# Reordered waits inside the head pairs, a spread of the side work, and identity products on TensorE in its idle stretches

## The chip, the cores and the metric

One core of a Trainium2 chip. The metric is the device time of the kernel in microseconds (us), the median of its runs. TensorE is the matmul engine (PE in the profile, PEld its weight loads), DVE is VectorE, ACT is ScalarE, POOL is GpSimd, SP is SyncE, which here only issues transfers.

## The reference

`x` is [4, 1024, 128] in float32. The block computes `x = x + attn(layernorm(x))`, where attn itself adds its input, and then `x = x + ffn(layernorm(x))`:

- attention: 16 heads of 64, `softmax(q k^T / 8) v` over 1024 keys for each batch and head, then the output projection, added to the normed input
- feed-forward: a mixture of 8 experts. `probs = softmax(x Wr)`, each of the 4096 tokens goes to its best expert, at most 512 tokens an expert in order of token number, `y = relu(xe W1) W2` times the token's probability (of the tokens of the second layernorm, which the branch adds to its result). Tokens beyond the 512 keep zero

```python
q = einsum('bsd,hdk->bhsk', x, w_q)      # k, v likewise
weights = softmax(einsum('bhqk,bhmk->bhqm', q, k) * scale, axis=-1)
z = einsum('bhqm,bhmk->bhqk', weights, v)
x = x + einsum('bse,ed->bsd', z, w_o)
rank = cumsum(onehot(argmax(probs))) ...  ; keep = rank < cap
```

## The kernel before, in words

**Tiling.** Two heads make a pair: 4 batches x 8 pairs = 32 pairs (`PAIRS`), walked in order by every engine (`in_order`, L243). A pair has 4 octets (`oct`); an octet is 8 tiles of scores (k = 0 to 7), each 128 keys x 512 queries of one head. Octets 0 and 1 are the first 512 queries (h = 0), octets 2 and 3 the second 512. For each tile TensorE makes the scores in one of three banks ps_s (`scores`, L1004 and L1005: two products, high and low parts), ScalarE writes the exponential into `ring` (`unit`, L583), GpSimd adds the tiles up over keys into `acc` (`add_up`, L444, one add of 128x1024 for two tiles), and TensorE multiplies the ring by V into ps_z (`values`, L1018) and later sums `acc` over partitions (`softmax_sums`, L1028).

**The maximum.** Before a pair's scores are used, the maximum over keys must be known: TensorE makes a cheap copy of the scores (`max_scores`, L970, called a visit, two per octet, numbered v) into the four banks of ps_m, DVE reduces them (`reduce_max`, L783), TensorE turns the maxima (`turn_max`, L989), ScalarE copies them to mxt (L563) and SP places them as a row of queriesB (`place_max`, L315). A visit uses all of ps_m, so everything else that needs PSUM borrows a part of ps_m between two visits and must be read out before the next: lent_qk (projections of q and k for the next pairs), lent_turn, lent_out (V's projection and the output projection), lent_max. In the code of TensorE the waits of those readers stand together in front of the visit (L1116 to L1138).

**The side work of an octet**, all inside the same order: `project_qk` (L949 to L951), `cast_qk` (ACT, L542), `low_qk` (DVE, L778), `place` (SP, L302 to L309), `project_v` and `copy_v` (L958, ACT L558) in octets 0 and 2, `project_out` (L1036) and `add_out` (DVE, L805) in octets 1 and 3, `recip` (DVE, L792, four quarters), `scale_z` (DVE, zT, L800). `split_high_weights` (ACT, L546) stands once in each pair, behind octet 0.

**Rarer work.** The tokens of a batch are split into a high and a low part (`split_high_tokens` on ACT L553, `split_low_tokens` on POOL L432) two pairs before the batch starts, in pairs 6, 14 and 22. `clear_slots` (ACT's queue, L529) fills the table of slots in HBM, in pair 1. The routing of batches 0 to 2 is spread over the pairs from 23 on by `routed(j, role)`, for batch b in pairs 23+2b (a: moments), 24+2b (b: second norm), 25+2b (c: turn, logits, choose, count_ranks, find_slots), 26+2b (d) and 27+2b (e: scatter of the rows, POOL L420, an indirect DMA for each 128 tokens). Batch 3 is routed behind the last pair. Then the experts follow (L1196 to L1234).

**Where the order comes from.** Everything is written out by hand: each engine's list of instructions in `pair(j, par, b)`, with semaphores that count.

```python
                    unit(j, oct, 3)
                    if oct in (0, 2) and not last:
                        copy_v(j + 1, nxt, oct // 2, lent_out)
                    unit(j, oct, 4)
```

Before the pairs, DVE finds the moments of batches 0 and 1, norms batch 0, sets constants and norms batch 1 (L713 to L722); the moments of batches 2 and 3 come right in front of the pairs (L873).

Of the kernel before, what the change touches and what calls it, by code (L numbers as in the profile page):

```python
# [28 lines left out]
def block_kernel(nc, x_in, w_q, w_k, w_v, w_o, w_r, w_1, w_2, out):  # L29
# [30 lines left out]
    with ExitStack() as ctx:  # L60
# [167 lines left out]
        def qk_bank(j, use):  # L228
            if isinstance(j, int) and j == 0:
                return ps_m[1 - use // 2][:, (use % 2) * HALF:(use % 2 + 1) * HALF]  # L230
            if isinstance(j, int) and j == 1 and use < 2:
                return ps_s[use][:, :]
            return lent_qk
# [3 lines left out]
        LAST_BY_PE = 2  # L237
        LAST = PAIRS - 1


        LOOPED = []

        def in_order(engine, pair):  # L243
            j = 0
            while j < PAIRS:
                looped = dict(LOOPED).get(j)
                if looped:
                    with engine.Fori(0, looped) as i:
                        for par in range(2):
                            pair(2 * i + j + par, par, j // HP)  # L250
                    j += 2 * looped
                else:
                    pair(j, j % 2, j // HP)
                    j += 1
# [6 lines left out]
        def routed(j, role):  # L261
            if not isinstance(j, int):
                return None
# [3 lines left out]
        def known(j, *which):  # L267
            return isinstance(j, int) and j in which

        @block.sync  # L270
        def _(sp):
# [5 lines left out]
            def load_weights(j, par):  # L277
                hp = j % HP
                view = wst[par][:, 0:4 * DK].rearrange("p (h t k) -> p h t k", h=2, t=2)
                sp.dma_start(view[:, :, 0, :], wq_d[:, bass.ds(2 * hp, 2), :]).then_inc(w_loaded[par], 16)  # L280
                sp.dma_start(view[:, :, 1, :], wk_d[:, bass.ds(2 * hp, 2), :]).then_inc(w_loaded[par], 16)
                sp.dma_start(wst[par][:, 4 * DK:6 * DK].rearrange("p (h k) -> p h k", h=2),
                             wv_d[:, bass.ds(2 * hp, 2), :]).then_inc(w_loaded[par], 16)
            def load_wo(j, par):
                sp.dma_start(wo[par][:, :].rearrange("p (o d) -> p o d", o=1),
                             wo_d[:, bass.ds(j % HP, 1), :]).then_inc(wo_loaded[par], 16)
# [78 lines left out]
        def _(pool):  # L365
# [64 lines left out]
            def split_low_tokens(b):  # L430
                pool.wait_ge(high_split, 2 * b + 2)
                pool.tensor_tensor(h_low[:, :], hT[:, b * S:(b + 1) * S], h_high[:, :].bitcast(F32),  # L432
                                   ALU.subtract).then_inc(low_split, 1)

            def add_up(j, h, kt):
                pool.wait_ge(exp_done, 2 * UNITS * j + UNITS * h + 2 * kt + 2)
                if kt == 1:
                    if not (isinstance(j, int) and j == 0):
# [818 lines left out]
```

## Time and profile before

| | |
|---|---|
| median of 3 runs | 1662.51 us (1659.98 to 1663.33) |
| the profiled execution, its own time | 1658.69 us |
| its span | 1656.9 us |
| TensorE busy (PE) | 1524.6 us, 92% |
| weight loads (PEld) | 870.7 us, 53% |
| VectorE, ScalarE, GpSimd busy | 1072.0 (65%), 811.3 (49%), 1189.6 us (72%) |
| the chain that ended last | PE 85%, DVE 4%, POOL 3% |
| mean granted clock of TensorE | 0.963 of full speed |

A page of the profile gives one execution: busy times, the costliest groups of instructions, and for each the idle time of its engine in front of them. The trace behind it can be asked for single instructions in order of time, for waits summed by pairs of lines, and for busy times in chosen stretches.

### The profile page before, as it was taken

The page shows a single profiled execution, that of the slowest core. Times are in us where ns is not written, and L with a number is a line of the kernel's source. Part 1 is how long each engine was busy: PE and PEld are TensorE (multiplying, and loading weights), DVE is VectorE, ACT ScalarE, POOL GpSimd, SP SyncE. Part 2 cuts the span into 40 slices and gives each one's busy share as a digit, 9 for nine tenths or more (in the row PEclk, how much of TensorE's full clock was granted, in tenths as well). Part 3 has the DMA queues.
Part 4 walks back from the last instruction along what each step waited for, and adds up shares of the span by engine and source line. Part 5 has one row for each costly group of instructions (what it writes and reads, how often), then busy time and mean ns, then how long its engine had stood idle before and what let it go on. Part 6 is the DMA issues. An engine that isn't in the chain of part 4 may idle for free.

```text
span 1656.9 us, 21749 instructions
## 1 busy us (share of the span) xinstructions
PE 1524.6 (92%) x7396; PEld 870.7 (53%) x7396; DVE 1072.0 (65%) x1316; ACT 811.3 (49%) x1586; POOL 1189.6 (72%) x687
## 2 busy tenths in 40 slices
PE   3798999999999999999999999999998989999376
PEld 1354555555555555555555555555564555554266
DVE  4665676666766666756677666667677767766332
ACT  1464555545455455455555555454554645545221
POOL 2586677777777777777777777777877868879225
PEclk8799999999999999999999999999999989999588
DMA  5345222333333332223333332322233322220531
GB/s 136 78 117 128 56 66 64 73 79 80 80 81 70 74 79 68 63 50 78 80 80 81 80 78 67 80 60 65 63 70 90 96 64 70 71 70 25 155 126 37
DMA packets 115342, 129.56 MB, mean 78 GB/s; under 512 B 40490, under 2 KB 65583, under 8 KB 115232
## 3 DMA queue, kind: packets, MB, share of 16 engines
q1 hardware_dynamic: 108512, 117.80, 30.3%
q0 software_dynamic: 2560, 6.14, 1.1%
q10 hardware_dynamic: 4160, 4.23, 1.1%
q8 instruction: 60, 0.98, 0.3%
q14 instruction: 50, 0.41, 0.1%
HBM read 18.91 MB, written 12.65 MB: 19 GB/s over the span
## 4 chain that ended last, share of the span: by engine, by line
PE 85%; DVE 4%; POOL 3%; ACT 2%; issue 2%; DMA 2%; SPq 1%; POOLq 0%; DVEq 0%; ACTq 0%
PE ps_z L1018 26%; PE ps_s L1004 15%; PE ps_s L1005 13%; PE ps_m L970 10%; PE ps_m L958 3%; PE ps_s L1028 3%; PE ps_m L1036 3%; ACT ring L583 2%; PE ps_m L949 2%; PE ps_m L950 2%; PE ps_m L951 2%; DVE mxw L783 1%; POOL acc L444 1%; PE ps_m L1211 1%; PE ps_z L1211 1%
## 5 line engine op out<-in xcount | busy, mean ns | idle before, releaser
L444 POOL TENSOR_TENSOR acc<-acc,ring 128x1024 f32<-128x1024 f32 x382 | 907.0, 2374 | 189.1 <-ACT ring L583 148.7
L783 DVE TENSOR_REDUCE mxw<-ps_m 128x1 f32<-128x1024 f32 x512 | 602.7, 1219 | 425.7 <-PE ps_m L970 424.0
L583 ACT ACTIVATE ring<-ps_s 128x512 f32<-128x512 f32 x1024 | 544.9, 600 | 122.5 <-PE ps_s L1005 120.7
L1018 PE MATMUL ps_z<-ring,V 128*64 128x512 f32 x2048 | 471.2, 602 | 0.0
L1004 PE MATMUL ps_s<-queriesA,keysA 128*128 128x512 f32 x1024 | 441.5, 431 | 16.7 <-ACT ring L583 13.8
L1005 PE MATMUL ps_s<-queriesB,keysB 65*128 65x512 f32 x1024 | 409.8, 400 | 0.0
L1018 PEld LDWEIGHTS ps_z<-ring,V 128*64 128x64 f32 x2048 | 136.6, 137 | 268.8 <-issue 240.4
L1004 PEld LDWEIGHTS ps_s<-queriesA,keysA 128*128 128x128 f32 x1024 | 196.3, 192 | 126.6 <-issue 48.0
L444 POOL TENSOR_TENSOR acc<-ring 128x1024 f32<-128x1024 f32 x64 | 152.8, 2388 | 145.0 <-ACT ring L583 145.0
L792 DVE RECIPROCAL sums<-sums 128x128 f32<-128x128 f32 x252 | 228.9, 930 | 8.7 <-ACT sums L574 8.7
L970 PE MATMUL ps_m<-keysA,queriesA 64*128 64x512 f32 x1024 | 190.9, 450 | 26.9 <-DVE mxw L783 9.8
L1005 PEld LDWEIGHTS ps_s<-queriesB,keysB 65*128 65x128 f32 x1024 | 197.0, 192 | 32.2 <-issue 0.8
L970 PEld LDWEIGHTS ps_m<-keysA,queriesA 64*128 64x128 f32 x1024 | 78.5, 188 | 179.3 <-issue 153.6
L574 ACT ACTIVATE sums<-ps_s 128x512 f32<-128x512 f32 x63 | 37.7, 598 | 266.2 <-PE ps_s L1028 266.2
L569 ACT ACTIVATE zr<-ps_z 128x512 f32<-128x512 f32 x64 | 38.3, 598 | 223.2 <-PE ps_z L1018 223.2
L778 DVE TENSOR_TENSOR qk_rest<-ps_m,qk_high 128x512 fp32r<-128x512 f32 x126 | 85.8, 682 | 46.8 <-ACT qk_high L542 29.8
L542 ACT ACTIVATE qk_high<-ps_m 128x512 fp32r<-128x512 f32 x126 | 75.4, 599 | 43.0 <-PE ps_m L951 23.0
L1036 PEld LDWEIGHTS ps_m<-wo,zT 128*128 128x128 f32 x512 | 67.8, 194 | 11.8 <-issue 6.0
L1036 PE MATMUL ps_m<-wo,zT 128*128 128x128 f32 x512 | 68.7, 277 | 4.3 <-DVE zT L800 4.3
L958 PEld LDWEIGHTS ps_m<-wst,hT 128*128 128x128 f32 x496 | 69.1, 202 | 6.2 <-DVE mxw L783 0.2
L958 PE MATMUL ps_m<-wst,hT 128*128 128x128 f32 x496 | 69.1, 285 | 0.0
L1028 PE MATMUL ps_s<-acc,ones 128*64 128x512 f32 x256 | 66.7, 593 | 0.0
(126 smaller groups left out, 916.6 us busy)
## 6 DMA issues: line engine op xcount, KB each, us to landing
queriesA<-qk_high SPq DMA_DIRECT2D x256, 128.0 KB, 2.3
keysB<-qk_high SPq DMA_DIRECT2D x128, 128.0 KB, 2.3
keysA<-qk_rest SPq DMA_DIRECT2D x128, 128.0 KB, 2.4
queriesB<-qk_rest SPq DMA_DIRECT2D x128, 128.0 KB, 2.4
keysA<-qk_high SPq DMA_DIRECT2D x96, 128.0 KB, 2.3
tokens_by_slot<-blank ACTq DMA_DIRECT2D x4, 1032.0 KB, 7.5
ring<-tokens_by_slot SPq DMA_DIRECT2D x8, 516.0 KB, 6.2
x<-in_L_attn_x SPq DMA_DIRECT2D x4, 512.0 KB, 6.4
```

The costliest lines, as they stand in the source:

```text
L444: pool.tensor_tensor(acc[h][:, :], before, P_both(kt), ALU.add).then_inc(summed, 1)
L583: act.activation(P_tile(kt, p), ps_s[k % 3][:, :], ACT.Exp, scale=SCALE).then_inc(exp_done, 1)
L778: dve.tensor_tensor(qk_rest[s][:, :], qk_bank(j, use), qk_high[s][:, :].bitcast(F32), ALU.subtract).then_inc(qk_low, 1)
L783: dve.tensor_reduce(mxw[h][:, p * HT + qt:p * HT + qt + 1], ps_m[p][:, :], AX_X, ALU.max).then_inc(maxed, 1)
L792: dve.reciprocal(sums[:, c], sums[:, c]).then_inc(recip_done, 1)
L958: mm = pe.matmul(bank[:, i * P:(i + 1) * P], hT[:, t:t + P], wst[par][:, 4 * DK:6 * DK], start=True, stop=True)
L970: mm = pe.matmul(ps_m[p][:, kh * HALF:(kh + 1) * HALF], queriesA[par][p][r, at:at + P], keysA[par][p][r, kh * HALF:(kh + 1) * HALF], start ...
L1004: pe.matmul(ps_s[k % 3][:, :], keysA[par][p][:, t], queriesA[par][p][:, c], start=True, stop=False)
L1005: pe.matmul(ps_s[k % 3][:, :], keysB[par][p][:, t], queriesB[par][p][:, c], start=False, stop=True).then_inc(scores_ready, 1)
L1018: mm = pe.matmul(ps_z[p * DK:(p + 1) * DK, :], V[par][:, kt * P + p * DK:kt * P + (p + 1) * DK], P_tile(kt, p), start=(kt == 0), stop=(kt ...
L1028: mm = pe.matmul(ps_s[2][p * DK:(p + 1) * DK, :], ones[:, :], part, start=(i == 0), stop=(i == len(parts) - 1))
L1036: mm = pe.matmul(bank[:, i * P:(i + 1) * P], zT[h][:, i * P:(i + 1) * P], wo[par][:, :], start=True, stop=True)
```

## The change

On TensorE: `spin(times)` multiplies the identity by itself into ps_s[1], 20 times before the first turn, 18 times behind the last sums, 38 times in front of the wait for the last output projection's add, 70 times behind the last batch's ranks. In the pairs:

- ACT: unit 4 comes before copy_v
- DVE: add_out comes before the second quarter of recip; `find_slots` (and TensorE's `count_ranks`) go from octet 3 of the pair with role c to octet 0 of the pair with role d, their second part behind that octet's reductions
- the tokens of a batch are split in two halves: behind octets 0 and 2 on ACT, in front of the add of kt = 5 of either half on POOL
- `clear_slots`: 16 stores of 256 rows in pairs 3 to 6 in place of 4 of 1024 rows in pair 1
- POOL: the 8 scatters of a batch stand 4 in the second half of role d and 4 in the first half of role e; before, 6 in d and 2 in e
- DVE: the moments of batch 2 come before the norm of batch 0, those of batch 3 behind it

A form with loops that was not in use is taken out. The diff, cut:

```diff
         LAST_BY_PE = 2
+        CLEAR_FROM, CLEARED = 3, 2 * P
...
+        SPLIT_IN = {0: 0}
+        SPLIT_IN.update((HP * b - 2, b) for b in range(1, B))
...
-                    pool.wait_ge(slots_cleared, 16 * (E * CAP // S))
+                    pool.wait_ge(slots_cleared, 16 * (E * CAP // CLEARED))
...
-            def split_low_tokens(b):
-                pool.wait_ge(high_split, 2 * b + 2)
-                pool.tensor_tensor(h_low[:, :], hT[:, b * S:(b + 1) * S], h_high[:, :].bitcast(F32),
+            def split_low_tokens(b, g):
+                pool.wait_ge(high_split, 2 * b + g + 1)
+                c, at = slice(g * HALF, (g + 1) * HALF), b * S + g * HALF
+                pool.tensor_tensor(h_low[:, c], hT[:, at:at + HALF], h_high[:, c].bitcast(F32),
                                    ALU.subtract).then_inc(low_split, 1)
...
-                        if known(j, 0) and (h, kt) == (0, 6):
-                            split_low_tokens(0)
-                        if known(j, *range(HP - 2, PAIRS - HP, HP)) and (h, kt) == (1, 1):
-                            split_low_tokens(b + 1)
+                        if j in SPLIT_IN and kt == 5:
+                            split_low_tokens(SPLIT_IN[j], h)
...
-                        if routed(j, "d") is not None and kt in (3, 5, 7):
-                            scatter(routed(j, "d"), [3 * h + kt // 2 - 1])
-                        if routed(j, "e") is not None and h == 0 and kt in (3, 5):
-                            scatter(routed(j, "e"), [6 + kt // 2 - 1])
+                        if routed(j, "d") is not None and h == 1 and kt % 2 == 1:
+                            scatter(routed(j, "d"), [kt // 2])
+                        if routed(j, "e") is not None and h == 0 and kt % 2 == 1:
+                            scatter(routed(j, "e"), [4 + kt // 2])
...
-            def split_high_tokens(b, last_use):
-                act.wait_ge(hT_ready, 2 * b + 2)
-                act.wait_ge(qk_done, last_use)
-                for g in range(2):
+            def split_high_tokens(b, g):
+                act.wait_ge(hT_ready, 2 * b + g + 1)
+                if b > 0:
+                    act.wait_ge(qk_done, 4 * HP * b - 2 + 2 * g)
...
                     unit(j, oct, 3)
+                    unit(j, oct, 4)
                     if oct in (0, 2) and not last:
                         copy_v(j + 1, nxt, oct // 2, lent_out)
-                    unit(j, oct, 4)
...
-                    if known(j, 0) and oct == 0:
-                        split_high_tokens(0, 0)
-                    if oct == 1 and known(j, *range(HP - 2, PAIRS - HP, HP)):
-                        split_high_tokens(b + 1, 4 * (j + 1) + 4)
+                    if j in SPLIT_IN and oct in (0, 2):
+                        split_high_tokens(SPLIT_IN[j], oct // 2)
...
-                    if known(j, 1):
-                        clear_slots(oct)
+                    if CLEAR_FROM <= j < CLEAR_FROM + E * CAP // CLEARED // OCTS:
+                        clear_slots(OCTS * (j - CLEAR_FROM) + oct)
...
-            for b in range(2):
+            for b in range(3):
                 for g in range(2):
                     first_moments(b, g)
             for g in range(2):
                 first_norm(0, g)
+            for g in range(2):
+                first_moments(3, g)
...
+                    if oct in (1, 3) and not first:
+                        add_out(j - 1, oct // 2, before, lent_out)
                     if oct == 1 and not first:
                         recip(j - 1, 1, 1)
-                        add_out(j - 1, 0, before, lent_out)
                     if oct == 3:
                         recip(j, 0, 1)
-                        if not first:
-                            add_out(j - 1, 1, before, lent_out)
...
-                    if routed(j, "c") is not None and oct == 3:
-                        find_slots(routed(j, "c"), 0)
+                    if routed(j, "d") is not None and oct == 0:
+                        find_slots(routed(j, "d"), 0)
...
-                    if routed(j, "c") is not None and oct == 3:
-                        find_slots(routed(j, "c"), 1)
+                    if routed(j, "d") is not None and oct == 0:
+                        find_slots(routed(j, "d"), 1)
...
-            for b in (2, 3):
-                for g in range(2):
-                    first_moments(b, g)
...
+            def spin(times):
+                for _ in range(times):
+                    pe.matmul(ps_s[1][:, 0:P], ident[:, :], ident[:, :], start=True, stop=True)
...
-                    pe.wait_ge(low_split, b + 1)
+                    pe.wait_ge(low_split, 2 * b + half + 1)
...
-                    if c is not None and oct == 3:
-                        count_ranks(c)
+                    if routed(j, "d") is not None and oct == 0:
+                        count_ranks(routed(j, "d"))
...
+            spin(20)
             for g in range(2):
                 turn_h(0, g)
...
             softmax_sums(LAST, 1, LAST_BY_PE)
+            pe.wait_ge(exp_done, UNITS * HALVES)
+            spin(18)
             project_out(LAST, 1, 1, lent_qk)
 
+            spin(38)
             pe.wait_ge(wo_added, 2 * PAIRS)
...
             count_ranks(B - 1)
+            spin(70)
```

## Rows read from the trace of the kernel before

**Rows 1.** List of waits: who waited for whom, us in total, times, longest.
```profile
PE ps_s L1004 <- ACT ring L583: 13.8, 51, 1.8
...
PE ps_m L970 <- issue: 7.7, 26, 0.3
```

**Rows 2.** Timeline, pair 4, octet 0: start us, us, engine, line, out<-in [idle before].
```profile
250.58 0.60 ACT L558 ACTIVATE V<-ps_m 128x512 f32<-128x512 f32 x1 [0.66 <-PE ps_m L958]
...
251.10 0.39 PE L1005 MATMUL ps_s<-queriesB,keysB 65*128 65x512 f32 x1
...
251.72 0.50 PE L1004 MATMUL ps_s<-queriesA,keysA 128*128 128x512 f32 x1 [0.23 <-ACT ring L583]
```

**Rows 3.** Timeline, pair 4, octet 1.
```profile
262.58 0.94 DVE L792 RECIPROCAL sums<-sums 128x128 f32<-128x128 f32 x1
...
263.44 0.63 DVE L805 TENSOR_TENSOR x<-ps_m,x 128x512 f32<-128x512 f32 x1
...
264.17 0.73 PE L970 MATMUL ps_m<-keysA,queriesA 64*128 64x512 f32 x4 [0.30 <-issue]
```

**Rows 4.** Timeline of ScalarE, the one L546 in pairs 1, 3, 6 and 7.
```profile
109.57 0.44 ACT L546 ACTIVATE w_high<-wst 128x256 fp32r<-128x256 f32 x1
...
207.90 0.45 ACT L546 ACTIVATE w_high<-wst 128x256 fp32r<-128x256 f32 x1
...
343.16 0.45 ACT L546 ACTIVATE w_high<-wst 128x256 fp32r<-128x256 f32 x1
...
391.87 0.45 ACT L546 ACTIVATE w_high<-wst 128x256 fp32r<-128x256 f32 x1
```

**Rows 5.** Timeline of TensorE: the matmuls behind its long pauses in pairs 1, 6, 26 and 30.
```profile
128.71 0.50 PE L1004 MATMUL ps_s<-queriesA,keysA 128*128 128x512 f32 x1 [2.92 <-DMA queriesB<-mxt]
...
362.74 0.58 PE L949 MATMUL ps_m<-h_high,w_low 128*128 128x512 f32 x1 [1.82 <-POOL h_low L432]
...
1256.02 0.79 PE L949 MATMUL ps_m<-h_high,w_low 128*128 128x512 f32 x1 [5.36 <-DVE mxw L783]
...
1453.55 0.50 PE L949 MATMUL ps_m<-h_high,w_low 128*128 128x512 f32 x1 [2.02 <-DVE mxw L783]
```

**Rows 6.** Stretches: us, busy us (count) of each engine, PEclk, DMA share, GB/s.
```profile
1253.80:1260.70 6.90, 4.68 (x16) 4.01 (x16) 4.55 (x7) 1.20 (x2) 2.15 (x2) 0.51 0.29 65
...
1540.60:1588.30 47.70, 13.39 (x56) 10.82 (x57) 13.97 (x47) 10.91 (x23) 12.37 (x25) 0.50 0.47 143
```

**Rows 7.** Timeline, GpSimd's adds and DVE's step beside them, pairs 25 and 30.
```profile
1247.10 7.38 POOL L444 TENSOR_TENSOR acc<-acc,ring 128x1024 f32<-128x1024 f32 x3
...
1252.31 2.19 DVE L768 TENSOR_TENSOR scatter_at<-routing_columns 128x8 int32<-128x8 f32 x1
...
1499.61 4.51 DVE L800 TENSOR_TENSOR zT<-sums,zr 128x512 f32<-128x512 f32 x1
```

**Rows 8.** Timeline, the end of the start.
```profile
52.52 0.88 DVE L694 BATCH_NORM_STATS2 moment_parts<-x 128x6 f32<-128x128 f32 x4
...
57.90 2.32 DVE L783 TENSOR_REDUCE mxw<-ps_m 128x1 f32<-128x1024 f32 x2
...
59.15 2.08 PE L945 MATMUL ps_m<-hT,wst 128*128 128x512 f32 x2 [3.06 <-DVE mxw L783]
```

**Rows 9.** Timeline, the last pair and what follows it.
```profile
1506.49 1.00 POOL L420 DMA_INDIRECT tokens_by_slot<-rows,scatter_at  x1 [0.15 <-POOL acc L444]
...
1523.77 10.18 POOL L444 TENSOR_TENSOR acc<-acc,ring 128x1024 f32<-128x1024 f32 x4
...
1542.08 2.04 PE L1036 MATMUL ps_m<-wo,zT 128*128 128x128 f32 x8 [4.31 <-DVE zT L800]
...
1557.46 3.56 PE L1050 MATMUL ps_m<-wr,hT 128*128 128x8 f32 x16 [0.84 <-ACT hT L496]
...
1582.91 1.09 PE L1201 MATMUL ps_m<-ident,ring 128*128 128x128 f32 x4 [19.42 <-DMA ring<-tokens_by_slot]
...
1593.73 3.73 PE L1211 MATMUL ps_z<-w,rT 128*128 128x128 f32 x32
```

More of the change, by code:

```diff
@@ L228, in qk_bank @@
         def qk_bank(j, use):
-            if isinstance(j, int) and j == 0:
+            if j == 0:
                 return ps_m[1 - use // 2][:, (use % 2) * HALF:(use % 2 + 1) * HALF]
-            if isinstance(j, int) and j == 1 and use < 2:
+            if j == 1 and use < 2:
                 return ps_s[use][:, :]
@@ L237, in block_kernel @@
         LAST_BY_PE = 2
+        CLEAR_FROM, CLEARED = 3, 2 * P
         LAST = PAIRS - 1
-        LOOPED = []
         def in_order(engine, pair):
[L244 to L254, printed above, removed]
+            for j in range(PAIRS):
+                pair(j, j % 2, j // HP)
+        SPLIT_IN = {0: 0}
+        SPLIT_IN.update((HP * b - 2, b) for b in range(1, B))
         ROUTE_FROM = PAIRS - 9
@@ L261, in routed @@
         def routed(j, role):
-            if not isinstance(j, int):
-                return None
             b, odd = divmod(j - ROUTE_FROM - "abcde".index(role), 2)
@@ L267, in known @@
         def known(j, *which):
-            return isinstance(j, int) and j in which
+            return j in which
         @block.sync
@@ L437, in add_up @@
                 if kt == 1:
-                    if not (isinstance(j, int) and j == 0):
+                    if not (j == 0):
                         pool.wait_ge(sums_done, 2 * j + h - 1)
@@ L528, in clear_slots @@
                 act.wait_ge(blank_ready, 2)
[L529 to L530 removed]
+                act.dma_start(slots_d[n * CLEARED:(n + 1) * CLEARED, :].rearrange("(p n) w -> p n w", p=P),
+                              blank[:, :].rearrange("p (o w) -> p o w", o=1).to_broadcast([P, CLEARED // P, W])
                               ).then_inc(slots_cleared, 16)
@@ L774, in low_qk @@
                 s = use % 2
-                if not (isinstance(j, int) and j == 0 and use < 2):
+                if not (j == 0 and use < 2):
                     dve.wait_ge(low_placed[s], 32 * (2 * j + use // 2))
@@ L809, in pair @@
                 first, last = known(j, 0), known(j, LAST)
-                before = (j - 1) // HP if isinstance(j, int) else b
+                before = (j - 1) // HP
                 for oct in range(OCTS):
@@ L964, in max_scores @@
                 at = h * HALF + qt * P
-                if not (isinstance(v, int) and v == 0):
+                if not (v == 0):
                     pe.wait_ge(maxed, 2 * v)
@@ L1067, in pair @@
                 first, last = known(j, 0), known(j, LAST)
-                next_b = (j + 1) // HP if isinstance(j, int) else b
-                second_b = (j + 2) // HP if isinstance(j, int) else b
+                next_b, second_b = (j + 1) // HP, (j + 2) // HP
                 for oct in range(OCTS):
@@ L1130, in pair @@
                             pe.wait_ge(logits_copied, c + 1)
-                        if c is not None and oct == 3:
-                            pe.wait_ge(ranks_read, c + 1)
+                        if routed(j, "d") is not None and oct == 0:
+                            pe.wait_ge(ranks_read, routed(j, "d") + 1)
                         if oct in (1, 3):
```

15 lines of the change are left out of this document (6 added, 9 removed).

## The prediction, made before the changed kernel ran

> **What bounds the kernel now.** I read the page first (its numbers are in the table above): TensorE is busy for 92% of the span and carries 85% of the chain that ended last, so only what lets TensorE start earlier, or run at its higher clock, counts. Then I asked how regular it is. One ScalarE instruction (L546) runs once per pair, at a fixed place; [rows 4] give its starts in pairs 1, 3, 6 and 7. Pairs 3 to 6 follow each other at (343.16 - 207.90) / 3 = 45.09 us. That is the undisturbed pair. Anything above it is a one-off stall, anything inside it is paid some 30 times. So the sum has two kinds of terms: small waits in every pair, and stalls in the few pairs that carry extra work.
>
> **Waits in every pair.** In an octet of 8 score tiles the last one starts 251.72 - 251.10 = 0.62 us after the instruction in front of it, where 0.23 is the step of a 512-column matmul [rows 2]: 0.39 lost. It needs a bank of ps_s whose exponential (unit 4) comes behind copy_v on ScalarE, and ScalarE stood idle 0.66 us in front of copy_v for TensorE's project_v. The list of waits counts 51 such waits [rows 1], one of them (the 1.8) another story, so 50. The change puts unit 4 in front of copy_v. Its scores are ready by then, it fits into the idle 0.66, and copy_v starts when it did. The end of copy_v (251.18) is then the next to be late, but TensorE asks for V only at its visit, 0.8 us later. Unit 5, behind copy_v, keeps its time. Gain 50 x 0.39 = 19.5; nothing at the other end, if something else holds that tile.
>
> In the second octet TensorE waits 0.30 us in front of its visit [rows 3], 26 times in the list [rows 1]. The 263.44 add (add_out) is what it needs, because lent_out is in a bank that the visit overwrites, and a reciprocal of 0.94 stands in front of that add. The change swaps them. The add can then start at 262.6, when the projection has just left TensorE, and ends before TensorE arrives; the reciprocal runs beside the visit (0.73 us and more). With the step lost at its start I count 0.36: 26 x 0.36 = 9.3. In the fourth octet the same swap finds no wait to remove: nothing. The new wait is for wo_done at the head of DVE's queue, with a reciprocal and a reduction behind it; the reduction has to wait for the visit anyway.
>
> **Stalls that go.** (a) clear_slots. Pair 1 issues four stores of 1032 KB from ScalarE's queue; the small move of the maxima into queriesB is then late and TensorE waits 2.92 us [rows 5]. From pair 1 to pair 3 the pitch is 98.33 [rows 4], 8.15 over two undisturbed pairs, the rest being a late placement in pair 2 and the slow clock behind it. The change makes 16 stores of a quarter of the size in pairs 3 to 6. A quarter of 2.92 is 0.7 in four pairs, but in part there is room: I take -8.1 and +1, between +0 and +4. The Trainium skill (Trainium Kernel Development and Optimization, Key Constraints) says that DMAs from several queues interleave on the same engines. By that alone the small move would not have been held up; the 2.92 says that it was.
>
> (b) The token split for the next batch. In pair 6 TensorE stands 1.82 us for h_low [rows 5], which GpSimd makes in one piece right before it is wanted. The pitch to pair 7 is 48.71 [rows 4], 3.62 too long: 1.82 waiting and 1.8 at a granted clock that fell during the pause. The pattern stands three times (pairs 6, 14, 22); once the clock holds. The change makes the first half a whole octet earlier and the second half in time for the next pair: 3 x 1.82 + 2 x 1.8 = 9.1 gone. It costs two more issues on ScalarE and GpSimd, both with room.
>
> (c) Routing of batches 0 to 2. The stall of 5.36 us at 1256.02 [rows 5] comes from DVE: find_slots stands in front of the reduction that TensorE waits for. Its tiny instructions took up to 2.19 us, and this one ended just as the third add of GpSimd's 7.38 us did [rows 7]. During the stall the clock fell: 4.68 us of matmuls at half clock [rows 6], so 2.3 more. This stands in pairs 26 and 28 (7.7 each); in pair 30 it is 2.02 and about 1.7 of clock. Sum 19. The change moves the step behind the visit of the next pair's first octet, where DVE has about 2.8 us until its next reduction while find_slots takes 1.5 us beside an idle GpSimd (in the tail) and 6 beside its adds. Next late is that reduction. Between no stall and 3 us each I take 1.1 each, because GpSimd has a pause of 2 us in that octet, and 1 us for the four scatters per half: -15.7 + 1 = -14.7. Four scatters in a half (before three and two) are otherwise covered by GpSimd's pauses in these pairs. The rule of the skill (SBUF — State Buffer, Who interferes with whom) is that DVE with two SBUF inputs and a GpSimd instruction that reads SBUF exclude each other for a whole instruction. The 2.19 agrees; zT's 4.51 [rows 7], longer than any one add, does not. By the rule three blocks of at most one add each could follow in the new place too, and the saving would be nearer 10.
>
> **Start.** DVE's moments for batches 2 and 3 leave the place before the pairs, where TensorE idles 3.06 us for the reduction at 57.90 [rows 8]. With the clock that fell there I count 3.06 + 1.7 = 4.8. They go in front of the norms of batches 0 and 1. Four halves took 57.90 - 52.52 = 5.38, or 1.35 each; the first two partly fall into DVE's wait for the roots, the others delay the first low_qk. Cost 1.6 us (between 0 and 5). The 20 identity products run in the wait for the first turn. If they keep the clock up, that is lost again in DVE's order: nothing. Sum -3.2.
>
> **Tail.** One product is 2 instructions. At high clock 3.73 / 32 = 0.117, at low clock 3.56 / 16 = 0.22 [rows 9], so 0.23 or 0.44 us a product. 18 of them are 4.2, behind the last sums, where TensorE idles 4.31; 38 are 8.9 in an idle of some 10; 70 are 16.4 (30.8 at low clock) in an idle of 19.42 [rows 9]. Now the clock is low from 1540.6 to 1588.3, with 13.39 us of matmuls [rows 6], of which some 8 lie on the path; half of that could be won. I take 3, between 0 and 4. Against it: GpSimd's adds are unbroken to the end, 1523.77 + 10.18 = 1533.95 [rows 9], when TensorE is ready for the last sums. Two more scatters of 1.0 stand in that row of adds now: +1.9. Net -1.1, between -4 and +10 (70 products at low clock would outlast their wait by about 10).
>
> **Sum.** -19.5 - 9.3 - 7.1 - 9.1 - 14.7 - 3.2 - 1.1 = -64. The profiled execution took 1658.7, so 1594.7; the median of the runs is 3.8 above that execution, so 1598.
>
> **Rivals.**
> - *The waits in every pair only move* (0.17). Another wait stands just behind: the tile's bank comes free and V, the add or a placement holds TensorE instead. For: several semaphores meet at the visit. Against: each is met 0.7 us or more earlier. The 29 us stay: 1627.
> - *Routing still stalls* (0.13). In the new octet find_slots meets GpSimd's adds and delays the reduction by 3 us or more, with the clock falling again. Then 12 of 15.7 stay: 1610.
> - *It does not do what it says* (0.03): the products fail to raise the clock and outlast their waits at 0.44 each; 70 are 11 us over, the other two about 10. With the 3 not won: 1622.
> - *Slower* (0.03). zT is in front of low_qk on DVE, and V's visit waits for low_qk. Once zT took 4.51 us [rows 7] because it met unbroken adds. Bare it is 0.7, so 3.8 late, less 1.5 of room: 2.3 us, twice a pair. If shorter octets bring zT into GpSimd's adds in all pairs, it is +140 and the time is about 1735. It decides when zT starts before GpSimd's last add of the half ends; now a pause of about 1 us lies between.
>
> **How the numbers follow.** Forecast 0.64, at 1598. A change of under 0.2% (3.3 us) can't be told from none. The range runs from the best ends (clears 1, routing 3, start 1.6, tail 3, and 4 for the median) to just short of the first rival: 1586 to 1624. Every case but the last ends faster by more than 3.3 us; for small misses together I leave 0.02 on no change. Faster 0.95, same 0.02, slower 0.03.
>
> **What would show it.** L546 at a pitch of 44.0 in quiet pairs; the L1004 and L970 waits of [rows 1] gone; a step of 0.23 at the last tile; no wait for mxt in pair 1 and none for h_low in 6, 14, 22; the stall in pairs 26 and 28 about 1 us; the last add on GpSimd 2 us later than TensorE; high clock in the tail's routing. I am wrong if the pitch stays near 45, or if TensorE's idle in pairs 24 to 31 is as large as now.

## The result and the profile after

The changed kernel took 1603.09 us (median of 4 runs, 1600.34 to 1604.84) against 1661.24 for the kernel before beside it: a ratio of 0.9648, 95% interval 0.9629 to 0.9666. In a later trial it was 0.9641 (0.9624 to 0.9658). The forecast was 1598.0, range 1586 to 1624. The time lies inside, but one large term of the sum failed, and another, which I had put too small, covered about half of it: the hit is in part luck.

| | before | after |
|---|---|---|
| the profiled execution, own time | 1658.69 us | 1604.84 us |
| span | 1656.9 us | 1602.8 us |
| TensorE busy | 1524.6 us, 92% | 1536.1 us, 96% |
| mean granted clock | 0.963 | 0.975 |

TensorE is busier although it does the same useful work: the identity products count as busy. So the share says little here, and I read waits and single instructions.

From the list of waits of the changed kernel (us in total, times, longest), and from the page the group of the scores' first matmuls, with the idle time in front of them at the end:

```profile
PE ps_m L961 <- DVE mxw L773: 9.8, 4, 2.4
PE ps_m L940 <- DVE mxw L773: 9.5, 3, 4.6
```

```profile
L995 PE MATMUL ps_s<-queriesA,keysA 128*128 128x512 f32 x1024 | 433.3, 423 | 0.4
```

L995 stood 13.8 us for its exponential in [rows 1] (L1004 there); now its whole idle is 0.4. The 26 waits of L970 are gone too. The 9.8 belongs to the start. The 9.5 is the stall of pairs 26, 28 and 30, which was to go.

Timeline, pair 4, octet 0, then octet 1:

```profile
236.51 0.60 ACT L548 ACTIVATE V<-ps_m 128x512 f32<-128x512 f32 x1
...
237.01 0.40 PE L996 MATMUL ps_s<-queriesB,keysB 65*128 65x512 f32 x1
237.24 0.40 PE L995 MATMUL ps_s<-queriesA,keysA 128*128 128x512 f32 x1
237.48 0.40 PE L996 MATMUL ps_s<-queriesB,keysB 65*128 65x512 f32 x1
...
248.00 0.68 DVE L795 TENSOR_TENSOR x<-ps_m,x 128x512 f32<-128x512 f32 x1
248.60 0.94 DVE L782 RECIPROCAL sums<-sums 128x128 f32<-128x128 f32 x1
...
249.24 0.73 PE L961 MATMUL ps_m<-keysA,queriesA 64*128 64x512 f32 x4
```

Beside [rows 2]: the step to the last tile is 0.23 (before 0.62), with 0.24 behind it. Beside [rows 3]: the add comes first and ends 0.56 before the visit, which waits for nothing.

ScalarE's one L536 (L546 before) in pairs 1, 3, 6 and 7:

```profile
106.42 0.42 ACT L536 ACTIVATE w_high<-wst 128x256 fp32r<-128x256 f32 x1
...
194.74 0.42 ACT L536 ACTIVATE w_high<-wst 128x256 fp32r<-128x256 f32 x1
...
326.11 0.42 ACT L536 ACTIVATE w_high<-wst 128x256 fp32r<-128x256 f32 x1
...
369.81 0.42 ACT L536 ACTIVATE w_high<-wst 128x256 fp32r<-128x256 f32 x1
```

Pair 7 follows pair 6 at 43.70 now, where [rows 4] had 48.71: the split of the tokens costs nothing. From pair 1 to pair 3 it is 88.32 (98.33 before). Pairs 3 to 6 stand (326.11 - 194.74) / 3 = 43.79 apart; of the 0.27 us above three times 43.70, 0.2 is in pair 4 alone. Most quiet pairs have 43.70, against the 45.09 of before.

Now the part that failed. Timeline of pair 26, octets 0 and 1: GpSimd, DVE, TensorE; and the stretch behind the pause (us, busy us and count of PE, PEld, DVE, ACT, POOL, then PEclk, DMA share, GB/s):

```profile
1205.68 2.36 POOL L436 TENSOR_TENSOR acc<-acc,ring 128x1024 f32<-128x1024 f32 x1
...
1208.19 2.39 POOL L436 TENSOR_TENSOR acc<-acc,ring 128x1024 f32<-128x1024 f32 x1
...
1211.23 2.33 POOL L436 TENSOR_TENSOR acc<-acc,ring 128x1024 f32<-128x1024 f32 x1
```

```profile
1206.05 2.07 DVE L752 TENSOR_TENSOR logits<-one_hot,logits 128x64 f32<-128x64 f32 x1
1208.15 0.22 DVE L753 TENSOR_REDUCE routing_columns<-logits 128x8 f32<-128x64 f32 x1
1208.41 2.19 DVE L755 TENSOR_SCALAR routing_columns<-routing_columns 128x8 f32<-128x8 f32 x1
...
1210.71 0.57 DVE L757 TENSOR_TENSOR routing_columns<-routing_columns 128x8 f32<-128x8 f32 x1
1211.32 2.26 DVE L758 TENSOR_TENSOR scatter_at<-routing_columns 128x8 int32<-128x8 f32 x1
...
1213.86 2.30 DVE L773 TENSOR_REDUCE mxw<-ps_m 128x1 f32<-128x1024 f32 x2
```

```profile
1215.09 0.79 PE L940 MATMUL ps_m<-h_high,w_low 128*128 128x512 f32 x1 [4.63 <-DVE mxw L773]
```

```profile
1211.00:1221.00 10.00, 5.91 (x18) 4.98 (x19) 7.46 (x10) 2.74 (x6) 4.92 (x3) 0.66 0.16 37
```

Three tiny instructions of find_slots take 2.07, 2.19 and 2.26 us, and each ends within 0.1 us of an add of GpSimd (1208.04, 1210.58, 1213.56). A fourth takes 0.57 and ends as GpSimd's short step for w_low does (1211.26). This part of find_slots lasts 7.9 us, the reduction behind it starts 5 us after its visit has ended, TensorE waits 4.63 us, and its clock is at half from 1214.2 to 1221.0. It is the picture of before [rows 5, 7], one octet later. An octet here is the time from its first exponential to the next octet's first:

| | before | after |
|---|---|---|
| pair 26, octets 0 and 1 | 19.56, 10.91 | 11.62, 18.18 |
| pair 28, octets 0 and 1 | 19.74, 10.92 | 11.63, 17.88 |
| pair 30, octets 0 and 1 | 15.16, 10.92 | 11.65, 11.07 |

The tail, from the last pair to the first tokens:

```profile
1466.57 10.15 POOL L436 TENSOR_TENSOR acc<-acc,ring 128x1024 f32<-128x1024 f32 x4
...
1476.78 1.78 PE L1019 MATMUL ps_s<-acc,ones 128*64 128x512 f32 x2 [0.99 <-POOL acc L436]
...
1482.09 4.29 PE L922 MATMUL ps_s<-ident 128*128 128x128 f32 x36
...
1500.44 3.14 PE L1041 MATMUL ps_m<-wr,hT 128*128 128x8 f32 x16 [0.84 <-ACT hT L486]
...
1525.43 0.63 PE L1196 MATMUL ps_m<-ident,ring 128*128 128x128 f32 x4 [1.16 <-DMA ring<-tokens_by_slot]
```

The unbroken adds end 1.9 us later behind the last exponential than in [rows 9], and TensorE stands 0.99 us for them and 0.80 for zT before. Its clock is low from 1477.0 to 1480.4. From the last exponential to the first tokens it is 54.4 us, 52.7 before. From there to the end it is 77.4 against 74.0, which the experiments settle below.

### The profile page after: what moved, and what is told of

Read it like the earlier page. It is cut to its first block, busy times and chain, and to the rows that moved or that the text cites. A ratio compares the mean times of both kernels' runs of the same rounds, so it can differ in the third digit from the quotient of the medians.

```text
span 1602.8 us, 22351 instructions
## 1 busy us (share of the span) xinstructions
PE 1536.1 (96%) x7688; PEld 904.4 (56%) x7688; DVE 1079.0 (67%) x1316; ACT 811.6 (51%) x1586; POOL 1189.5 (74%) x691
## 4 chain that ended last, share of the span: by engine, by line
PE 86%; DVE 5%; POOL 4%; issue 1%; SPq 1%; DMA 1%; ACT 1%; another core or an unknown queue 0%; POOLq 0%; DVEq 0%; ACTq 0%
PE ps_z L1009 26%; PE ps_s L995 15%; PE ps_s L996 14%; PE ps_m L961 10%; PE ps_m L949 3%; PE ps_s L1019 3%; PE ps_m L1027 3%; POOL acc L436 3%; PE ps_m L940 2%; PE ps_m L941 2%; PE ps_m L942 2%; DVE mxw L773 1%; PE ps_z L1206 1%; POOL tokens_by_slot L411 1%; PE ps_m L1206 1%
## 5 line engine op out<-in xcount | busy, mean ns | idle before, releaser
L995 PE MATMUL ps_s<-queriesA,keysA 128*128 128x512 f32 x1024 | 433.3, 423 | 0.4
L995 PEld LDWEIGHTS ps_s<-queriesA,keysA 128*128 128x128 f32 x1024 | 195.7, 191 | 88.6 <-issue 45.4
L961 PEld LDWEIGHTS ps_m<-keysA,queriesA 64*128 64x128 f32 x1024 | 77.5, 187 | 170.1 <-issue 145.8
L949 PEld LDWEIGHTS ps_m<-wst,hT 128*128 128x128 f32 x496 | 65.5, 192 | 5.9 <-DVE mxw L773 0.2
L949 PE MATMUL ps_m<-wst,hT 128*128 128x128 f32 x496 | 65.8, 275 | 0.0
```

What stands on the lines that cost most here:

```text
L949: mm = pe.matmul(bank[:, i * P:(i + 1) * P], hT[:, t:t + P], wst[par][:, 4 * DK:6 * DK], start=True, stop=True)
L961: mm = pe.matmul(ps_m[p][:, kh * HALF:(kh + 1) * HALF], queriesA[par][p][r, at:at + P], keysA[par][p][r, kh * HALF:(kh + 1) * HALF], start ...
L995: pe.matmul(ps_s[k % 3][:, :], keysA[par][p][:, t], queriesA[par][p][:, c], start=True, stop=False)
```

## The experiments

Twelve kernels ran, 1 to 4 on one chip, 5 to 8 on a second and 9 to 12 on a third. Each is compared with the kernel before on its own chip.

**1. find_slots back at its old place.**

```diff
-                    if routed(j, "d") is not None and oct == 0:
-                        find_slots(routed(j, "d"), 0)
+                    if routed(j, "c") is not None and oct == 3:
+                        find_slots(routed(j, "c"), 0)
```

(and so its second part and count_ranks)

> The changed kernel, but find_slots and count_ranks stand in octet 3 of pair c again, as before the change. The stall did not go with the move: pairs 26 and 28 lost 7.8 and 7.9 us in octet 0 before, and 7.6 and 7.3 in octet 1 after; only pair 30 fell from 3.7 to 0.5. Theory A (the place changes nothing while GpSimd's adds lag there): about 1606 us, that is 3 to 4 slower than the changed kernel, with octet 0 of pairs 26 and 28 at 18.5 to 19.5 and octet 1 at 10.55 again. Rival B (the new place is worse than the old one once the pairs are shorter): 1598 or less. Rival C (the old place is much worse): over 1610.

Measured: 1599.66 us, ratio 0.9639 (0.9623 to 0.9655), that of the changed kernel. Octet 0 of pairs 26 and 28 is 18.98 and 19.28, octet 1 is 10.55 again; pair 30's octet 0 is 13.16. The stall is there at either place: theory A. Over pairs 25 to 30 the octets are 2.9 us longer at the old place (without a dip of the clock in pair 27), which the ratios can't separate from nothing; the median is low because the experts' stretch is 3.4 us shorter on this chip (runs 9 to 11).

**2. No identity products.** The four calls of spin are left out.

> The changed kernel without any identity product (the 20, 18, 38 and 70 are left out, the orders stay). Theory A (the products in the tail are worth their clock): low clock from the last sums to the experts' first tokens, 3 us or more lost in the tail, the start the same within 0.5 us: 1606 to 1608. Rival B (they are worth nothing or harm, since the stretch from the tokens to the end got 3.4 us longer although the clock is high): 1600 to 1603, the expert cadence at 7.2 us again instead of 7.6 to 7.7. Rival C (the 20 at the start carry pair 0): first exponential more than 1 us later.

Measured: 1601.38, ratio 0.9655 (0.9638 to 0.9672); beside run 1, on the same chip, 1.7 us slower in the median, which the intervals do not separate. By these two traces, the clock is low for 48 us of the tail instead of 13.6, the first tokens come 54.5 us behind the last exponential instead of 53.1, and the rest is 74.6 instead of 73.7: 2.4 us. That size is not firm. With two scatters in the last pair the first tokens come at 50.3, 51.6 and 51.9 in three kernels with products (runs 9 to 11, 3 and 12) and at 51.8 to 52.8 in four without, and run 4, without products and on this chip, has a rest of 73.7. So about 1 us to the tokens is what all traces carry. Run 1 is also no clean partner: between first and last exponential it is 2.8 us longer, for find_slots' old place. The experts' pace is 7.2 us in both. So the long expert stage is not explained by the products, and run 1 has them without it. In the start, x landed 0.6 us later in this kernel, which is most of the 0.7 that its first exponential is later. This hardly is chance: DVE's first instruction, which waits for x, starts at 4.67 to 4.86 us in all nine kernels with products and at 5.28 to 5.40 in all five without, though x is asked for at 0.8 in each. Why stays open.

**3. The scatters in the order of before** (six in pair d, three in each half; two in pair e).

```diff
-                        if routed(j, "d") is not None and h == 1 and kt % 2 == 1:
-                            scatter(routed(j, "d"), [kt // 2])
+                        if routed(j, "d") is not None and kt in (3, 5, 7):
+                            scatter(routed(j, "d"), [3 * h + kt // 2 - 1])
```

> The changed kernel with the scatters spread as before it: six in pair d (three in each half) and two in pair e, so that the last pair issues two instead of four. Theory A: GpSimd's last add ends 1.9 to 2.1 us earlier and the tail is 2 to 3.5 us shorter (with the clock that falls in that wait); but three scatters now stand in the first half of pairs 26 and 28, where find_slots has just ended late, and wait there for its index in front of the adds, which costs 0 to 4 us in each: 1599 to 1608. Rival B: the scatters do not set the last add, and the tail stays at 131.8 us from the last exponential to the end within 0.5.

Measured: 1580.84, ratio 0.9524 (0.9508 to 0.9539): about 20 us faster than the changed kernel. I had it on record that the scatters would cost time in the first half of the pair; they gain. Octet 1 of pairs 26 and 28 is 10.93 (18.18 and 17.88). Timeline of the same moment as above, GpSimd and DVE:

```profile
1210.31 1.19 POOL L411 DMA_INDIRECT tokens_by_slot<-rows,scatter_at  x1 [2.25 <-issue]
```

```profile
1205.98 2.07 DVE L752 TENSOR_TENSOR logits<-one_hot,logits 128x64 f32<-128x64 f32 x1
1208.09 0.22 DVE L753 TENSOR_REDUCE routing_columns<-logits 128x8 f32<-128x64 f32 x1
1208.34 0.17 DVE L755 TENSOR_SCALAR routing_columns<-routing_columns 128x8 f32<-128x8 f32 x1
...
1208.82 0.17 DVE L758 TENSOR_TENSOR scatter_at<-routing_columns 128x8 int32<-128x8 f32 x1
...
1209.27 2.31 DVE L773 TENSOR_REDUCE mxw<-ps_m 128x1 f32<-128x1024 f32 x2
```

The same L755 and L758 that took 2.19 and 2.26 take 0.17. GpSimd stands still for 2.25 us. The profile puts that down to issue, but by the code its scatter, in front of the add of kt 3, waits for the index that find_slots makes (last instruction at 1209.15), and so keeps the next add out of find_slots' way; run 5 tests that reading. In the tail the adds end 4.0 us behind the last exponential instead of 5.7, and the first tokens come at 51.6.

**4. Unit 4 in front of copy_v, alone, in the kernel before.**

```diff
+                    unit(j, oct, 4)
                     if oct in (0, 2) and not last:
                         copy_v(j + 1, nxt, oct // 2, lent_out)
-                    unit(j, oct, 4)
```

> The kernel before with one edit alone: unit 4 in front of copy_v on ScalarE. It removes the wait of 0.39 us at the last tile of octets 0 and 2. Theory A (the prediction's): steady pair 45.09 - 0.78 = 44.31, octets 0 and 2 at 11.41, about 20 us off: 1641. Theory B (the wait cost more than its length, for TensorE lost its stride too: octets 0 and 2 fell by 0.50 in the changed kernel): octets at 11.30, steady pair 44.09, 25 us off: 1636. Rival C (another wait takes its place as long as the add is not swapped): less than 10 us off.

Measured: 1632.59, ratio 0.9833 (0.9817 to 0.985), 26 us. Octets 0 and 2 are 11.30, the quiet pair 44.07: theory B. Beside [rows 2] one sees the missing 0.1. After the wait, L1004 took 252.06 - 251.72 = 0.34 us to the next matmul. In this kernel the step is 0.24 (first the line of before, then two of this run):

```profile
252.06 0.40 PE L1005 MATMUL ps_s<-queriesB,keysB 65*128 65x512 f32 x1
...
250.09 0.40 PE L1004 MATMUL ps_s<-queriesA,keysA 128*128 128x512 f32 x1
250.33 0.39 PE L1005 MATMUL ps_s<-queriesB,keysB 65*128 65x512 f32 x1
```

A wait cost its length plus 0.1 us in the step behind it; 51 of the 52 waits of L1004 in the kernel before have that step. That rest is the reason isn't shown: the same 0.34 stands once per octet behind the visit, where the profile has no wait.

**5. The changed kernel, with GpSimd waiting for find_slots** and the scatters four and four. This parts the two readings of run 3, the order of the scatters and the wait that it brings.

```diff
+                        if routed(j, "d") is not None and (h, kt) == (0, 3):
+                            pool.wait_ge(index_ready, routed(j, "d") + 1)
                         add_up(j, h, kt)
```

> The changed kernel, scatters four and four as it has them, with one wait more: GpSimd waits for find_slots' last result in front of its add of kt 3 in the first half of pair d. Theory A (find_slots is slow because each of its instructions waits for one of GpSimd's unbroken adds; the old scatter order helped by 20 us only because its first scatter made GpSimd wait for find_slots at exactly that place): find_slots falls from 8 us to about 3, octet 1 of pairs 26 and 28 from 18.2 and 17.9 to 10.9, the time to 1583 to 1587, all but the tail's 2 of the 20. Rival B (it is the number or the place of the scatters, four in one half): nothing changes, 1600 to 1603. Rival C (the stall only needs GpSimd behind, so a wait on GpSimd makes the adds later and exponentials wait for them): octets longer elsewhere, over 1590.

Measured: 1586.03, ratio 0.954 (0.9521 to 0.9559). Octet 1 of pairs 26 and 28 is 10.92 and 10.91. GpSimd, then DVE:

```profile
1208.25 2.38 POOL L436 TENSOR_TENSOR acc<-acc,ring 128x1024 f32<-128x1024 f32 x1 [1.37 <-DVE rows L763]
```

```profile
1204.79 2.07 DVE L754 TENSOR_TENSOR logits<-one_hot,logits 128x64 f32<-128x64 f32 x1
...
1207.15 0.17 DVE L757 TENSOR_SCALAR routing_columns<-routing_columns 128x8 f32<-128x8 f32 x1
```

One added wait of 1.37 us, on an engine off the critical path, takes away a stall of 7 us, in pair 26 and in pair 28. That is shown, and rival B falls.

**6. The same wait at the old place** (run 1, and GpSimd waits in front of its add of kt 6 in the second half of pair c).

> find_slots and count_ranks at their old place (octet 3 of pair c), scatters four and four, and GpSimd waits for find_slots' last result in front of its add of kt 6 in the second half of pair c. Theory A (the overlap with GpSimd's adds is the whole stall, the place of find_slots does not matter): pairs 26 and 28 lose their 7.7 us in octet 0, 1583 to 1588. Rival B (at the old place the reduction in front of the next visit is late anyway, since find_slots stands directly in front of it): 2 us or more stay in each of the pairs, 1588 or more.

Measured: 1589.07, ratio 0.9558 (0.954 to 0.9577). Octet 0 of pairs 26 and 28 is 12.51 and 12.49 (18.98 and 19.28 without the wait). Both are right in part: the wait is worth most of the stall, and 0.9 us beyond the 11.62 of the new place stay in octet 0, with 0.6 in the octet before, as the reduction stands directly behind find_slots. Over pairs 25 to 30 the new place is 3.6 us better, once GpSimd keeps away; a dip of the clock in pair 27 is not counted in that.

**7. Four score tiles of the last half summed by TensorE** (LAST_BY_PE = 4, in the kernel of run 3).

> The changed kernel with the scatters of before (the kernel that took 1580.8), and in the last half of the last pair TensorE sums four score tiles itself instead of two, so GpSimd has two adds of 2.4 us less. Theory A (GpSimd's adds set the start of the last sums, 5.8 us behind the last exponential): the sums start at about 1.5 us and take 1.3 us longer, 2.5 to 4 us off: 1577 to 1578.5. Rival B (the same time is lost in front of the next step, or to the clock): within 1 us of 1580.8.

Measured: 1588.64, ratio 0.9555 (0.9536 to 0.9573), slower than run 3. My expectation was wrong. (This run is on the second chip. Of some 5 us between the ratios, 3.2 are dips of the clock in pairs 27 and 29, so by the traces the price of the edit is the 2.9 by which the first tokens come later.) The adds do end 5.5 us earlier, before the last exponential does. But TensorE is busy with values and the projection until 3.9 us behind it, and the sums, eight matmuls more, end 3.2 us later than in run 3:

```profile
1462.32 1.07 PE L1019 MATMUL ps_s<-acc,ones 128*64 128x512 f32 x2
...
1465.80 3.65 PE L1019 MATMUL ps_s<-ring,ones 128*64 128x512 f32 x10
...
1469.38 4.29 PE L922 MATMUL ps_s<-ident 128*128 128x128 f32 x36
```

With two scatters in the last pair, GpSimd and TensorE come to the last sums within 0.3 us of each other. With four, GpSimd is 1.9 late.

**8. add_out in front of the reciprocal, alone, in the kernel before.**

```diff
+                    if oct in (1, 3) and not first:
+                        add_out(j - 1, oct // 2, before, lent_out)
```

> The kernel before with one edit alone: add_out in front of the reciprocal on DVE. Theory A (the prediction's 0.36): octet 1 from 10.92 to 10.55, the steady pair 45.09 to 44.72, and nothing in octet 3, which is 10.55 already; about 10 us off. Rival B (the wait only moves, to octet 2 or 3): less than 3 us off.

Measured: 1653.77, ratio 0.995 (0.9934 to 0.9967). Octet 1 is 10.55 and the quiet pair 44.72 (45.09): theory A.

**9 to 11. The changed kernel again, a better start, and that without products,** all on one chip. The start takes run 3's kernel and reorders DVE:

```diff
-            for use in range(4):
-                low_qk(0, use)
+            low_qk(0, 0)
+            low_qk(0, 1)
+            for g in range(2):
+                first_norm(1, g)
+            low_qk(0, 2)
...
+            low_qk(0, 3)
```

with two memsets of keysB behind low_qk 2, two behind low_qk 3, and the moments of batch 3 behind the first two visits' reductions; before, all of them stood in front of the first low_qk.

> The changed kernel once more, on one chip with the next two. In half of the profiles so far every expert but the first three takes 7.5 to 7.7 us instead of 7.2 and the stretch from the first tokens to the end 77.5 us instead of 73.5 to 74. Theory A: that belongs to the chip (all kernels of one call had it, or none), not to the change, so this run has it together with the two below, or all three are free of it; the ratio stays 0.964 to 0.966. Rival B: the change itself brings it, and only this kernel shows it.

> The changed kernel with the scatters of before (the kernel at 0.9524), and one more order at the start: on DVE the first two low_qk come first, and the norm of batch 1, the memsets of keysB and the moments of batch 3 fill its waits for the moves behind them. Now low_qk starts at 23.9 us though its input is cast by 18.1; in front of it stand 2.6 of moments, 4.3 of memsets and 2.1 of norm. Theory A (that order holds the start): low_qk at about 18.5, the first exponential 4 to 5.5 us earlier, at about 50, the ratio 0.949 to 0.950. Rival B (the fillers only move the wait: each placed one delays the next low_qk or reduction): 1 to 2 us earlier. Rival C (the first turns of batch 1 come late in pair 0): the gain is lost in pair 0.

> The same as start_first without the identity products. Without them, in the first trial, the clock was low for 48 us from the last sums on instead of 14, the tokens came 1.5 us later and the rest took 0.9 longer. Theory A: the products are worth 2 to 3 us, all of it in the tail, and this kernel is slower than start_first by that. Rival B (they are worth less than a measurement can tell, since TensorE mostly waits there): within 1 us.

Measured: the changed kernel 1602.71, ratio 0.9641 (0.9624 to 0.9658). Its stretch from the tokens to the end is 77.1 us, that of the other two 76.8 and 77.2. It was 73.4 to 74.6 in all of runs 1 to 4 and 77.5 to 77.9 in all of 5 to 8, the kernel before with the swapped add among them. So the 3.4 us don't belong to the change. They go with the chip, or with the time of the trial, which the runs don't part; on which chip the first two profiles (74.0 and 77.4) ran is not on record. The profile shows where they sit: DVE's last outputs wait for something that the trace puts outside the core. In the experts' stretch of the changed kernel's first profile, then of run 1:

```profile
L466 POOL DMA_INDIRECT out<-ye,ring x32 | 31.1, 971 | 46.3 <-DVE ye L885 38.3 <-issue 8.0
...
L885 DVE SCALAR_TENSOR_TENSOR ye<-ps_m,ring 128x128 f32<-128x128 f32 x16 | 4.5, 342 | 6.2 <-remote 6.2
```

```profile
L466 POOL DMA_INDIRECT out<-ye,ring x32 | 31.1, 973 | 42.3 <-DVE ye L885 35.0 <-issue 7.3
...
L885 DVE SCALAR_TENSOR_TENSOR ye<-ps_m,ring 128x128 f32<-128x128 f32 x16 | 4.5, 342 | 2.5 <-PE ps_m L1206 2.5
```

The instructions are as long in both; only what stands between them differs. Why stays open.

start_first: 1580.06, ratio 0.9516 (0.9499 to 0.9533), 22.6 us under the changed kernel on the same chip. The first low_qk starts at 18.31 (23.9 before), the first exponential at 51.4 (55.0): 3.6 us, a little under theory A. That the fillers delay the later steps somewhat is a likely reason, not tested.

start_first_no_spin: 1584.43, ratio 0.9545 (0.9524 to 0.9565), 4.4 us slower in the median. The profiled executions are 5.9 apart: 2.3 in the tail as in run 2 (1.9 to the tokens, 0.4 behind them), 0.7 x landing late again, 0.8 a first octet of 13.00 instead of 12.25, and 1.6 a dip of the clock in pair 27. The intervals overlap a little. Rival B (within 1 us) falls by the medians. Theory A's 2 to 3 us fit, but not all of it is in the tail, and start_first's tail is the shortest of its kind (run 2), so the products' price stays between about 1 and 4 us.

**12. Products in the start's waits too** (into ps_z, behind the first five max_scores).

```diff
                 max_scores(v, 0, v // 4, v % 4)
+                if v == 0:
+                    pe.wait_ge(v_copied, 2)
+                spin(5 if v < 2 else 8, ps_z)
```

> start_first with 34 more identity products, 5, 5, 8, 8 and 8 of them in TensorE's five waits of 2.45 us for the reductions behind the first max_scores. In start_first the clock is low from 29.9 to 53.8 us; a max_scores takes 1.22 us there and 0.73 at high clock, the first octet 12.25 instead of about 11.7. Theory A (unbroken work brings the clock back): 5 products at low clock are 2.2 us and fill the wait, the clock rises by the third visit, the first exponential comes 1 to 2 us earlier than 51.4 and the first octet is 0.5 shorter: ratio 0.9500 to 0.9510. Rival B (the clock stays low and 8 products at 0.44 us outlast the wait by 1.1 us each): 3 us later, ratio 0.953. Rival C (DVE's pace holds the start whatever TensorE does): the clock rises and the first exponential moves by less than 0.5.

Measured: 1578.44, ratio 0.9505 (0.9485 to 0.9524), the fastest of all. TensorE:

```profile
31.58 2.50 PE L928 MATMUL ps_z<-ident 128*128 128x128 f32 x10
34.09 1.22 PE L967 MATMUL ps_m<-keysA,queriesA 64*128 64x512 f32 x4
35.24 1.77 PE L928 MATMUL ps_z<-ident 128*128 128x128 f32 x10
37.76 0.74 PE L967 MATMUL ps_m<-keysA,queriesA 64*128 64x512 f32 x4 [0.74 <-DVE mxw L766]
```

The clock is low from 29.3 to 36.1 us, where it was low until 53.8 in start_first. A visit's matmuls fall from 1.22 to 0.74, the first exponential comes at 49.3 and the first octet is 11.41. The trace shows 2.1 + 0.8 = 2.9 us; the interval of the ratio overlaps that of start_first, so the ratio alone could not tell it. The two profiled executions are equally long, since this one has a dip of the clock in pair 25 (1.6) and a tail 0.9 longer.

## Why the prediction was right, and where it was not

- **Tile wait (predicted -19.5).** Right in its mechanism, too small: 50 x 0.50 = 25 in place of 50 x 0.39. The missing 0.1 is in [rows 2], in the step behind the waiting matmul; I subtracted one step where two were long. Run 4 shows that both go with the wait.
- **add_out (-9.3).** Right: octet 1 lost 0.37 us in some 24 pairs, -8.8 (in pairs 26 and 28 the stall hides it), and run 8 has it alone.
- **clear_slots (-8.1 + 1).** Over the quiet pair, pairs 1 and 2 were 8.2 us too long and are 0.9 now: -7.3. The stores in pairs 3 to 6 cost nothing that shows: pair 4 is 0.2 longer here but 43.74 in run 9, and pair 11, which has no store, is 0.2 longer too. No run has this edit alone. I was also wrong to set the sharing of the DMA engines against the delay: beside the store a move into queriesB landed after 6.2 us, elsewhere after 2.4, and sharing is reason enough for that.
- **Token split (-9.1).** Pairs 6, 14 and 22 were 3.6, 3.4 and 2.0 over 45.09; now none is over 43.70. -9.0, read from the pitches, with no run of its own.
- **Routing (-15.7 + 1).** This step failed. Against the octets of run 5, octet 1 of pairs 26, 28 and 30 is 7.3, 7.0 and 0.5 too long, 14.8 in all, where 19 stood before: 4.3 gained, and 1.5 more around it, mainly in octet 3 of pairs 25, 27 and 29, which find_slots has left. -5.8. The false sentence was "GpSimd has a pause of 2 us in that octet". It has one in quiet pairs. In pairs 26 and 28 GpSimd comes out of the root of role a (16 small instructions, 1191.09 to 1195.55) with its adds behind, and adds without a break; in pair 30, with no role a in front, the step was short. The Trainium skill (SBUF — State Buffer, Who interferes with whom) was right where I weighed it down: by that rule I wrote that three blocks of one add each could follow, and three followed, with a short fourth. It also says that tensor_scalar can contend (in its two-port modes) and tensor_reduce never does; L755 took 2.19, and no reduction of find_slots over 0.22. The zT of 4.51 in [rows 7], which I held against the rule, outlasted two adds in a row (their ends: 1501.24 and 1503.55) and ended 0.57 behind the second, so it fits too. The rival *Routing still stalls* is what happened in this part.
- **"1 us for the four scatters per half".** I priced them as work for GpSimd. What the old order gave was a wait: with the first scatter in front of kt 3, GpSimd would have stood aside for the moved find_slots. The change took that away in the same stroke, and so moved a step to a good place and left it unprotected. By the octets that is 14.8 us; by the ratio of run 5 (0.954 against 0.9641 and 0.9648) 17 to 18. The rest can't be put down to it: 1.6 is a dip of the clock in pair 27, which runs 6 and 11 have without the stall and runs 1 and 2 lack with it, and 1.5 a shorter first octet.
- **Start (-3.2).** The pause of 3.06 is gone; the first exponential came 0.4 later, not 1.6, and the first octet gained 2.5 beside the tile wait: -2.1. This size is loose: the first octet takes 12.2 to 13.7 us in the eight traces with this start and 16.7 to 17.6 in the three with the old one. It stayed at low clock until 60.5, which I had counted as won.
- **Tail (-1.1).** The 1.9 for the two scatters came, and the products won some 1 to 2.4 against the 3 predicted (run 2). But in this execution and in run 9 the clock fell behind the waits for zT and the adds, and the last sums ran 1.7 us longer; I had not priced that. Runs 1, 5 and 6 have the same waits (0.99 for the adds) and kept the clock. To the tokens +1.7. The 3.4 behind them are not the change's.

The profiled execution went from 1658.69 to 1604.84, 53.9 off. The terms give -25 - 8.8 - 7.3 - 9.0 - 5.8 - 2.1 + 1.7 + 3.4 = -52.9. The sum forecast 1594.7 for it: 8.9 of routing were missing, the tail was 2.8 and the start 1.1 worse and the experts' stretch took 3.4, against 5.5 more from the tile wait. That the sum of these misses stayed inside the range is luck. The medians are only 5.1 apart (1603.1 and 1598.0), because the execution profiled before lay 3.8 below its median and the one after 1.8 above. The pitch of quiet pairs (forecast 44.0, came 43.70) and the missing waits ruled out the rival that the waits only move; zT took 1.1 to 2.4 us in 10 of 64 cases, but TensorE waited for it in the tail only (0.80), so the slower case never came.

## What to carry to other kernels

When a chain of tiny VectorE instructions runs long, look whether each ends as a GpSimd instruction ends. If so, make GpSimd wait for the chain's last result: 1.4 us of waiting there gave back 7 on TensorE. Before moving a step or a scatter, list what its waits hold back besides the work itself, because an order can be doing a job that no line of it states. Price a wait at its length, plus the longer step behind it (0.1 us here), plus the clock if it falls: it did not fall behind each wait of the same length.

## What the runs showed of the hardware that was not expected

- Behind 51 of the 52 waits of L1004 in the kernel before, the next matmul came after 0.34 us instead of 0.24. The same step stands behind the visit in each octet, without a recorded wait.
- Between two unbroken adds of GpSimd, DVE got one or two tiny instructions through, then was held for a whole add again (2.07 to 2.26 us).
- With identity products in TensorE's waits of 2.45 us, the stretch at 1.2 GHz ended at 36.1 us of the span instead of 53.8. Ten of the 34 had been issued by then.
- x landed 0.6 us earlier in all nine kernels with identity products than in all five without.
- The experts' stage was 3.4 us longer on two chips of the three than on the third, each tried at its own time, with instructions of equal length.
